# A short memset behind each indirect transfer of the ranking and attention stages

## What is computed

```python
q = (x @ q_w.T + q_b).reshape(n, HEADS, HEAD_DIM)      # k and v likewise
scores = einsum('ehd,ehd->eh', q[row], k[col]) / sqrt(HEAD_DIM)
scores = scores + edge_emb @ eb_w.T + eb_b
seg_max = segment_max(scores, row)
exp_scores = exp(scores - seg_max[row])
attn = exp_scores / (segment_sum(exp_scores, row)[row] + 1e-10)
out = segment_sum(attn[..., None] * v[col], row).reshape(n, HIDDEN)
return layernorm(x + out @ out_w.T + out_b)
```

## Time and profile before

| | us |
|---|---|
| median of 3 timed runs (2775.1 to 2778.55) | 2776.0 |
| span of the profiled execution, first to last instruction | 3660.3 |

### The profile page before, as it was taken

The page is one execution under the profiler, slowest core; times in us unless marked ns, Lnnn a source line. Parts: engine busy times, 40 slices in busy tenths (PEclk is TensorE's granted clock), DMA queues, the critical chain, the costliest instruction groups (busy, mean ns, idle before and its releaser), DMA issues. The chain is left out here.

```text
span 3660.3 us, 55107 instructions
## 1 busy us (share of the span) xinstructions
PE 2329.8 (64%) x15474; PEld 1795.1 (49%) x15475; DVE 1675.0 (46%) x4581; ACT 1041.2 (28%) x2249; POOL 1820.6 (50%) x1841
## 2 busy tenths in 40 slices
PE   5878877787887888778255455555555545555524
PEld 4756555565655555555244444444444444444413
DVE  6753333333333333333255555555555555555585
ACT  0002212121222221212134343444434434343413
POOL 4225555455555555455544455544444445545454
PEclk9997777777787777777566766766676666666755
DMA  4211111111111111111133323322322233223523
GB/s 165 53 45 45 39 39 39 44 39 39 45 39 39 44 40 39 44 33 38 56 72 73 73 73 73 72 72 71 72 72 72 72 73 73 73 69 73 65 42 81
DMA packets 143792, 217.95 MB, mean 60 GB/s; under 512 B 40177, under 2 KB 100511, under 8 KB 143485
## 3 DMA queue, kind: packets, MB, share of 16 engines
q0 software_dynamic: 70528, 133.75, 15.4%
q1 hardware_dynamic: 60203, 74.08, 7.2%
q10 hardware_dynamic: 13018, 9.60, 1.0%
HBM read 188.81 MB, written 28.48 MB: 59 GB/s over the span
## 5 line engine op out<-in xcount | busy, mean ns | idle before, releaser
L966 POOL DMA_INDIRECT attend_kv<-kv_rows,attend_rec x880 | 842.6, 958 | 856.8 <-DVE attend_wv L1165 600.6
L669 POOL DMA_INDIRECT sorted_records<-rank_record,rank_row x832 | 809.2, 973 | 721.1 <-DVE rank_row L826 477.9
L989 PE MATMUL attend_key_ps<-attend_key_t,shift 64*64 64x1 f32 x220 | 36.8, 235 | 750.2 <-ACT attend_key_t L1090 744.1
L805 DVE TENSOR_TENSOR rank_picked<-rank_slot_ps,rank_hot_hi 128x416 f32<-128x416 f32 x104 | 93.3, 897 | 890.3 <-remote 792.7
L989 PEld LDWEIGHTS attend_key_ps<-attend_key_t,shift 64*64 64x64 f32 x220 | 30.7, 197 | 766.4 <-issue 766.4
L1017 PE MATMUL attend_sum_ps<-attend_wv,attend_hot 128*128 128x136 f32 x1760 | 399.9, 400 | 5.6 <-DVE attend_wv L1165 5.6
L1017 PEld LDWEIGHTS attend_sum_ps<-attend_wv,attend_hot 128*128 128x128 f32 x1760 | 365.0, 298 | 22.0 <-issue 7.1
L699 PE MATMUL rank_next_ps<-rank_hot_hi,rank_hot_lo 128*128 128x416 bf16 (+3 forms) x832 | 365.7, 598 | 0.0
L731 PE MATMUL rank_bias_ps<-rank_edges_t,w_eb 128*64 128x128 f32 x1664 | 298.9, 354 | 94.5 <-ACT rank_edges_t L769 72.2
L1256 DVE TENSOR_TENSOR attend_score<-attend_score,attend_seg_ps 128x64 f32<-128x64 f32 x110 | 24.3, 221 | 695.6 <-remote 691.3
L731 PEld LDWEIGHTS rank_bias_ps<-rank_edges_t,w_eb 128*64 128x64 f32 x1664 | 266.3, 185 | 124.4 <-issue 124.4
(11 more groups left out here) (261 smaller groups left out, 4401.0 us busy)
## 6 DMA issues: line engine op xcount, KB each, us to landing
rank_edges<-in_edge_attr SPq DMA_DIRECT2D x103, 512.0 KB
attend_kv<-kv_rows,attend_rec POOLq DMA_INDIRECT x880
sorted_records<-rank_record,rank_row POOLq DMA_INDIRECT x832
sorted_records<-prepare_blank POOLq DMA_DIRECT2D x8, 888.0 KB, 12.2
attend_rec<-sorted_records SPq DMA_DIRECT2D x110, 64.0 KB
merge_rows<-prepare_zero POOLq DMA_DIRECT2D x2, 1800.0 KB, 24.9
kv_rows<-prepare_kv_out ACTq DMA_DIRECT2D x9, 320.0 KB
finish_add<-merge_rows SPq DMA_DIRECT2D x1, 2880.0 KB, 14.3
```

Source lines behind the costliest of these rows:

```text
L669: pool.indirect_dma_start(rec_dram[:, :], bass.IndirectOffsetOnAxis(ap=row[:, u, t:t + 1], axis=0), record[:, u, t, :], None).then_inc(sca ...
L966: pool.indirect_dma_start(kv[:, v, t, :], None, kv_dram[:, :], bass.IndirectOffsetOnAxis(ap=rec[:, v, t, H + 2:H + 3], axis=0)).then_inc(k ...
```

## The change

Behind each indirect transfer of the two loops POOL writes zeros into 256 words of one partition of a new tile, `pace`. The partition is 0, 32, 64 or 96 in turn (`32 * (t % 4)`), and the cells are one of four rows of 256 words, two for even steps and two for odd ones. No other instruction reads or writes the tile. Each memset adds 1 to a new semaphore, `paced`. From the third step on POOL first waits until the memsets of two steps back are done, since those wrote the same cells. There are 832 memsets in ranking and 880 in attention. Nothing is removed or moved.

```diff
--- before.py
+++ after.py
@@ rank
+        pace = sb("pace", [P, 4, 256], F32)
+        paced = sem("paced")
@@ rank, block.gpsimd
             def step(k, u):
                 s = 2 * k + u
+                if not first(k):
+                    pool.wait_ge(paced, G * (s - 1))
                 pool.wait_ge(rows_ready, s + 1)
                 pool.wait_ge(meta_kept, s + 1)
                 pool.wait_ge(bias_kept, s + 1)
@@
                 for t in range(G):
                     pool.indirect_dma_start(rec_dram[:, :], bass.IndirectOffsetOnAxis(ap=row[:, u, t:t + 1], axis=0),
                                             record[:, u, t, :], None).then_inc(scattered[u], 16)
+                    pool.memset(pace[32 * (t % 4):32 * (t % 4) + 1, 2 * (u) + t // 4, :], 0.0).then_inc(paced, 1)
@@ attend, block.gpsimd
             def step(k, v):
                 s = 4 * k + v
+                if not early(k, v):
+                    pool.wait_ge(paced, G * (s - 1))
                 if not (fixed(k) and k == 0):
                     pool.wait_ge(weighted, s - 3)
                 pool.wait_ge(rec_in[v], 16 * (k + 1))
@@
                     pool.indirect_dma_start(kv[:, v, t, :], None, kv_dram[:, :],
                                             bass.IndirectOffsetOnAxis(ap=rec[:, v, t, H + 2:H + 3], axis=0)
                                             ).then_inc(kv_in[v], 16)
+                    pool.memset(pace[32 * (t % 4):32 * (t % 4) + 1, 2 * (v % 2) + t // 4, :], 0.0).then_inc(paced, 1)
```

## The result

The changed kernel takes 3025.8 us (median of 4 runs, 3024.9 to 3026.5) against 2776.8 us (4 runs, 2775.1 to 2778.6) for the kernel before: a ratio of 1.090, 95% interval 1.088 to 1.091, 249 us more. The direction was forecast; the forecast size, 86 us, was a third of it.

The account below looks back on a forecast made before the run. The prediction took GpSimd to bound attention, and PE and GpSimd to share ranking. Its terms, 75 us in attention, 10 in ranking and 1 for last landings, sum to 86 us, so 2862 us, range 2775 to 3160 us.

Parts of the forecast that it names:

- the late results: Both loops of the profile: PE's results reach other engines 4 to 8 us late per step; mostly absent from timed runs.
- The sign that I named for it: Profile of the changed kernel: its span should stay within 1% of 3660 us, unlike the timed runs.
- My period of 10.8 us: Both loops, timed runs: (2776 − 465)/214 = 10.8 us per step, with GpSimd coming close to that.
- The price of a memset: Behind each transfer: likely 0.03 to 0.25 us, taken as 0.085 us, or 0.7 us per batch of 8.
- Attention: Attention loop: GpSimd is the bound, so its longer batch counts in full, 110 × 0.7 = 75 us.
- Ranking: Ranking loop: the longer batch mostly hides under PE's step of 9.6 to 11.2 us; 0 to 73 us, taken as 10.
- my own case: Whole kernel: attention bound by GpSimd, a memset costs 0.03 to 0.15 us; 2790 to 2950 us, chance 0.49.
- A: Rival on memset price: one partition costs as much as 128, 0.25 us each; 3060 to 3205 us, chance 0.28.
- B: Rival: no change, GpSimd not the bound or the memset fits the 0.30 us gap; 2776 us, chance 0.17.
- D: Rival: low memset price, 0.03 us each, 26 us in attention; 2800 us, the low end of the main case.
- C: Rival: breaks between transfers let PE's results through, so the kernel gets faster; 2690 to 2770 us, chance 0.06.
- The added waits: GpSimd's wait for memsets of two steps back: taken as 0, at most 0.30 us per step, 64 us in all.

Follow-up runs that it names:

- short_attend: Kernel before, without memsets, with 6 gathers per attention step in place of 8 from the fifth step on; 2564.2 against 2781.3 us (0.922).
- before_again: The kernel before, without an edit, profiled once more; 3691.6 us, as the other runs of the kernel before in that set (3691.5).
- p128: Changed kernel with memsets of 256 words on all 128 partitions instead of one; +233 us against the kernel before, ratio 1.083.
- w1: Changed kernel with memsets of 1 word instead of 256 in both loops; +4 us against the kernel before, ratio 1.0018.
- rank_only: Changed kernel with the memsets and added wait taken out of attention, left in ranking alone; 2900.9 against 2779.3 us for the kernel before (1.043).
- lump_b: Changed kernel with the 8 memsets behind the batch's 8 transfers, not one behind each; lump's two measurements: 3280.9 against 3691.5, 3302.8 against 3704.3 us (kernel before).

## Why the prediction was wrong, step by step

*What bounds the kernel: half right, with a wrong reason.* That the timed runs lack the late results, and that GpSimd is then the bound of attention, held (`short_attend`, −217 us). The reason given, that most of the lateness "belongs to the profiled execution alone", is wrong: where it is seen, all timed runs have it too (`before_again`). The sign that I named for it, a profile of the changed kernel within 1% of 3660 us, was missed with 3023.2 us. The conclusion survived because it was drawn from the 2776 us of the timed runs themselves; for a late chip it would have been false. My period of 10.8 us was right for both loops, 10.80 and 10.94.

*The price of a memset: the term that was mis-sized.* I took 0.085 us, the geometric middle of 0.03 and 0.25; it is 0.20. The upper end, a memset's length by its words, supposed that one partition costs as much as 128, and I had no row for that; `p128` shows that it does (0.33 us, against 0.30 on one). The gap of 0.30 us I had only as nothing or as a whole one more; in fact 0.20 us of it stays around the memset (0.04 and 0.16) and the memset fills 0.10. Nor do only the memsets on partition 0 cost, those behind t = 0 and 4: the median distances in ranking are 1.47 to 1.51 us behind every t, where they were 1.276.

*Attention: 75 us forecast, 123 measured.* With 0.20 us, "its longer batch counts in full" would give 110 × 1.6 = 176 us. It doesn't count in full, because 0.42 us per step of standstill behind VectorE goes away. That cover wasn't in my list; in the first profile it is all but invisible, since no gather there meets attend_wv and the longest of 880 has 1.11 us.

*Ranking: 10 us forecast, 122 measured.* The mechanism, a batch hidden under PE's step, was right, and in the untouched loop PE is at 100%. Its size was off: PE's step is 10.8 us, so it hides 0.45 us of GpSimd's work and not up to 1.0. With 1.6 us added, 1.15 × 104 = 120 us stick out. Had the price been my 0.7 us per batch, (0.7 − 0.45) × 104 = 26 us would have.

*The sum* by measured terms: ranking 104 × (1.6 − 0.45) = 120, attention 110 × (1.6 − 0.42) = 130, together 250 us; measured 249. Both covers were read from the traces of these same loops, so this is bookkeeping that closes and not a forecast that came true.

*The rivals.* 3026 us lies between my own case (2790 to 2950) and A (full price, 3060 to 3205), in neither. A was nearer: its mechanism held, with 0.20 us in place of its 0.25. B and D fell on prompt chips. C, that breaks between transfers let PE's results through, was given 0.06 and has no part in the time on a prompt chip, where nothing waits for "remote". On late chips the kernel does get faster, with results 3 us late in place of 7 at L1266, but breaks of one word do nothing; C is neither shown nor ruled out there. No run shows the 2690 to 2770 us that the forecast gives it: with breaks of one word (`w1`) a prompt chip took 2783.4 us against 2779.3.

*The added waits* of GpSimd cost nothing: with one-word memsets and both waits in place the time is +4 us in all, at the edge of what can be measured.

## What to carry to other kernels

When a profile and the timed runs disagree by more than the change is worth, find out first whether the timed runs next to the profile are as long as it, and take the periods of a loop from a kernel that leaves that loop alone. A memset put behind an indirect transfer of GpSimd costs its own length less what fits into the gap that is there anyway (about 0.10 of 0.30 us here); its length goes by its words (0.09 us for one, 0.30 for 256, 0.52 for 512) and hardly by its partitions (0.33 us for 256 words of 128). A batch that is hidden is hidden only by the difference of two periods, so measure that difference (here 0.45 us) before calling an addition free.

## What the runs showed of the hardware that was not expected

- The same kernel took 2777 to 2781 us on some chips and 3690 to 3719 us on three others. On the latter VectorE goes on 4 to 8 us behind PE's result in 98 of 110 steps of attention and in 55 of 104 of ranking, in attention mostly 1.5 to 1.8 us after GpSimd's last gather of the batch has ended (`before_again`); more work for GpSimd shortens the total there (3691 to 3281 us with lumped memsets). The cause is open.
- An indirect gather of GpSimd that starts during a VectorE instruction with two SBUF inputs takes longer by what is left of it less 0.12 to 0.14 us (141 of 142 in `rank_only`). The 29 that start less than 0.18 us ahead of L1172 took 2.04 to 2.22 us; the longest of 880, which starts 0.21 us ahead, took 2.26 us in place of 0.96. The products, sums and scans, with one SBUF input, hold none (193 gathers, at most 0.97 us), and a memset is not held (91 of them, at most 0.32 us).
- A memset of one word behind a transfer is free (`w1`, ratio 1.0018); one of 256 words takes 0.30 us on one partition and 0.33 us on 128 (`p128`).
- Memsets of one partition in a row follow each other after (2.81 − 0.30)/7 = 0.36 us at 256 words, more than each one's 0.30 us (`lump_b`).
